# One step of attention and channel mixing, its instructions put in another order on every engine

## The chip, the cores and the metric

The kernel runs on one core of a Trainium2 chip. A core has a matrix engine (TensorE, PE in the profile), a vector engine (VectorE, DVE), an activation engine (ScalarE, ACT), a general engine (GpSimd, POOL) and SyncE (SP), which here only issues transfers. Each engine takes its own instructions in the order in which the program lists them, and waits at an instruction until the semaphores that it names have reached their values. The metric is the device time of one launch in microseconds, the median of several runs.

## The reference

The input `x` is 4096 tokens of 256 features. One layer of attention (16 query heads in 4 groups, head size 16, each token sees itself and the 127 before it) is followed by a residual sum and a layer norm; then a channel mix, again with residual and layer norm.

```python
q = (x @ Wq + bq);  k = (x @ Wk + bk);  v = (x @ Wv + bv)
scores = einsum(q, k) / sqrt(16)
scores = where((i - 128 >= j) | (i < j), -1e9, scores)
x = layernorm(x + softmax(scores) @ v @ Wo + bo)
x_prev = x shifted by one token
xr = mu_r * x + (1 - mu_r) * x_prev;  xk = mu_k * x + (1 - mu_k) * x_prev
r = sigmoid(xr @ W_r.T);  k_act = square(relu(xk @ W_k.T))
out = layernorm(x + r * (k_act @ W_v.T))
```

## The kernel before, in words

The 4096 tokens are 32 blocks of 128 (index `t`), four blocks to a superblock (index `s`, place `j` from 0 to 3). Queries and keys are split into bf16 parts, written to DRAM (`q_parts`, `k_parts`), and read back stacked in another layout (`qs`, `ks`).

A software pipeline runs over the blocks. In step `t` the engines work on seven blocks at once:

- block `t+2`: its key windows are copied (`window_copy`, four pieces, ScalarE) and its queries are tiled (`tile_q`, VectorE, waits for the stacked `qs`);
- block `t+1`: row maxima of the scores (`max_scores` 0 to 5 on TensorE, `tile_max` 0 to 5 and `turn_max` on VectorE), sent as two rows into `qs` by SyncE (`max_in`);
- block `t`: eight score products (`score` 0 to 7, TensorE, two banks in turn), eight exponentials (`exps`, ScalarE), eight triangular masks (`mask`, GpSimd); `x_plus_bo`;
- block `t-1`: product with the values (`values`, TensorE, needs all eight masks), `att_t_copy`, `turn_back`, `normalise`, `turn_attention`, `att_c_copy`;
- block `t-2`: `output_product`, `first_residual` with its moments, `first_rstd` (GpSimd), `first_norm` (ScalarE), `turn_x2`, `x2_t_copy`;
- block `t-3`: `difference` (GpSimd), `mixed`, `r_product`, `tanh`, `k_product`, `relu`, `square`;
- blocks `t-4` and `t-5`: `second_product`, `gate`, `second_residual`, `second_rstd`, then `second_norm` and `store`.

A projection of a later superblock is spread over the four steps in three pieces, `project_chunk` 0 and 1 at j = 3 and 2 at j = 0, with `v_turn` at j = 1; each piece brings a `high_part` and a `middle_part` on ScalarE, a `rest_part` on VectorE, a `low_part` on GpSimd and spills on SyncE, and after them come the stacks, `stack_k` and `stack_q`.

The order is written out by hand: each engine has a function `step` whose calls are its order in a step, and a function `finish` for what is left after the last step. `run` calls `step` for every block but the last (31, named `LAST`) and then `finish`. Two orders matter in what follows. On ScalarE (lines 829 to 878) the exponentials 0 to 3 stand together, then two window copies, and the output norm `second_norm` stands after the fourth window copy. On TensorE (lines 1455 to 1507) `k_product` comes after `score` 6 and waits for `tanh`; `second_product` comes after `max_scores` 1 and waits for `square`.

## Time and profile before

| quantity | value |
|---|---|
| median of 3 runs | 392.55 us (391.89 to 393.45) |
| the profiled execution | 394.04 us, its span 392.2 us |
| busy share of the span: PE, DVE, ACT, POOL | 93%, 84%, 86%, 74% |
| mean granted TensorE clock | 0.978 of full speed |

The span is the time from the first instruction to the last of this execution. The pipeline fills until about 60 us and drains from about 350 us; between them the same four steps repeat. In that stretch three engines are busy almost without a pause, so a share alone doesn't tell which of them sets the pace: the starts of their instructions must be read one after another, since durations overlap (a matmul's 0.38 us begins 0.22 us after the one before it).

### The profile page before, as it was taken

What the parts mean: (1) busy time and instruction counts of PE and PEld (TensorE: products, weight loads), DVE (VectorE), ACT (ScalarE), POOL (GpSimd) and SP (SyncE); (2) the same over time, 40 slices, a digit from 0 to 9 for tenths busy, and PEclk for the clock granted to TensorE, in tenths of its full rate; (3) what the DMA queues carried; (4) which work ended last, traced back from release to release, by engine and by line L of the source; (5) the groups of instructions that cost most, each with busy time, mean ns of one, the idle gap of its engine ahead of it and who ended that gap; (6) DMA issues with size and microseconds to landing.
All of it is one profiled execution on the core that took longest, in us unless ns stands there. A gap on an engine that the chain in (4) does not pass through costs nothing.

```text
span 392.2 us, 8166 instructions
## 1 busy us (share of the span) xinstructions
PE 365.8 (93%) x2339; PEld 228.1 (58%) x2340; DVE 327.7 (84%) x860; ACT 339.0 (86%) x697; POOL 290.8 (74%) x485
## 2 busy tenths in 40 slices
PE   8855889999999999999999999999999998998974
PEld 5432346666566666666566666666566666665552
DVE  6366767999899989999799989999899988997664
ACT  3346999999999999999999999999999998986753
POOL 3704777787699778987699768887699777788733
PEclk9995799999999999999999999999999999999998
DMA  7846587622965347622954257531764252000001
GB/s 260 172 110 125 111 212 164 116 41 56 166 154 80 80 71 180 119 58 55 182 137 97 64 87 187 99 73 42 131 142 94 55 96 55 16 15 18 27 15 40
DMA packets 51244, 39.24 MB, mean 100 GB/s; under 512 B 33088, under 2 KB 42880, under 8 KB 51072
## 3 DMA queue, kind: packets, MB, share of 16 engines
q1 hardware_dynamic: 50240, 36.91, 44.2%
q10 hardware_dynamic: 960, 1.81, 1.8%
q8 instruction: 19, 0.31, 0.3%
q14 instruction: 25, 0.20, 0.2%
HBM read 26.38 MB, written 12.06 MB: 98 GB/s over the span
## 4 chain that ended last, share of the span: by engine, by line
PE 62%; ACT 20%; DMA 6%; DVE 5%; issue 4%; SPq 2%; POOL 1%; POOLq 0%; DVEq 0%; ACTq 0%
PE av_ps L1332 13%; PE score_ps L1312 10%; PE gen L1351 8%; PE gen L1422 7%; PE proj_ps L1229 6%; ACT probs L696 5%; PE max_ps L1294 5%; DMA qs<-q_parts 3%; PE gen L1409 3%; PE gen L1392 3%; ACT windows L711 2%; ACT x L731 2%; ACT out_t L769 2%; ACT act_k L761 2%; PE av_ps L1367 1%
## 5 line engine op out<-in xcount | busy, mean ns | idle before, releaser
L510 POOL TENSOR_SCALAR_AFFINE_SELECT probs<-probs 128x512 f32<-128x512 f32 x252 | 164.8, 671 | 53.1 <-ACT probs L696 51.8
L696 ACT ACTIVATE probs<-score_ps 128x512 f32<-128x512 f32 x252 | 142.6, 593 | 14.9 <-PE score_ps L1312 14.0
L973 DVE TENSOR_REDUCE neg_max<-max_ps 128x3 f32<-128x480 f32 x146 | 88.6, 631 | 13.0 <-PE max_ps L1294 12.7
L1312 PE MATMUL score_ps<-qs,ks 98*128 98x512 bf16 x252 | 88.2, 390 | 4.8 <-ACT probs L696 2.6
L711 ACT COPY windows<-ks 96x640 bf16<-96x640 bf16 x124 | 86.9, 727 | 0.0
L1332 PE MATMUL av_ps<-probs,vals 128*32 128x512 f32 x488 | 59.9, 606 | 0.0
L1014 DVE SCALAR_TENSOR_TENSOR mix<-diff,first,x_t 128x128 f32<-128x128 f32 x128 | 52.9, 456 | 3.2 <-POOL diff L538 3.2
L1294 PE MATMUL max_ps<-windows,q_tiles 128*128 128x160 bf16 x420 | 50.5, 237 | 3.3 <-DVE q_tiles L965 2.3
L1294 PEld LDWEIGHTS max_ps<-windows,q_tiles 128*128 128x128 bf16 x420 | 36.0, 99 | 23.4 <-issue 4.5
L1312 PEld LDWEIGHTS score_ps<-qs,ks 98*128 98x128 bf16 x252 | 21.3, 98 | 41.7 <-issue 30.4
L517 POOL TENSOR_TENSOR rstd<-var,minus_half 128x1 f32<-128x1 f32 x64 | 35.5, 555 | 9.9 <-DVE var L997 9.7
L1351 PE MATMUL gen<-rest_w,act_k 128*128 128x256 f32 x128 | 35.5, 400 | 2.1 <-ACT act_k L761 1.3
L1422 PE MATMUL gen<-rest_w,att_c 128*128 128x256 f32 x128 | 34.3, 390 | 1.8 <-ACT att_c L721 1.8
L498 POOL TENSOR_TENSOR parts<-rest,parts 128x512 bf16<-128x512 f32 (+1 forms) x24 | 26.6, 1111 | 12.1 <-ACT parts L675 12.0
L1229 PE MATMUL proj_ps<-x_t,first 128*128 128x512 f32 (+1 forms) x76 | 35.1, 584 | 0.0
L1409 PEld LDWEIGHTS gen<-mix,rest_w 128*128 128x128 f32 x224 | 28.1, 191 | 8.9 <-issue 8.2
L1409 PE MATMUL gen<-mix,rest_w 128*128 128x128 f32 x224 | 30.7, 280 | 0.0
L992 DVE BATCH_NORM_STATS2 stats<-y 128x6 f32<-128x256 f32 x64 | 27.4, 428 | 2.2
L1392 PE MATMUL gen<-rest_w,mix 128*128 128x256 f32 x112 | 28.8, 379 | 0.0
L1332 PEld LDWEIGHTS av_ps<-probs,vals 128*32 128x32 f32 x488 | 12.6, 109 | 26.7 <-issue 22.8
L538 POOL TENSOR_TENSOR diff<-x_t 128x256 f32<-128x256 f32 x32 | 19.6, 613 | 11.0 <-DVE x_t L1004 7.7
L1351 PEld LDWEIGHTS gen<-rest_w,act_k 128*128 128x128 f32 x128 | 21.9, 189 | 8.0 <-ACT act_k L761 5.7
(112 smaller groups left out, 612.7 us busy)
## 6 DMA issues: line engine op xcount, KB each, us to landing
q_parts<-parts SPq DMA_DIRECT2D x42, 128.0 KB, 2.2
out<-out_t SPq DMA_DIRECT2D x32, 128.0 KB, 2.3
qs<-q_parts SPq DMA_DIRECT2D x7, 576.0 KB, 7.1
x_t<-x_feat SPq DMA_DIRECT2D x7, 512.0 KB, 9.3
x_in<-x_nat SPq DMA_DIRECT2D x7, 512.0 KB, 3.7
ks<-k_parts SPq DMA_DIRECT2D x42, 80.0 KB, 3.3
qs<-q_parts SPq DMA_DIRECT2D x8, 384.0 KB, 8.4
qs<-q_parts SPq DMA_DIRECT2D x14, 192.0 KB, 6.1
```

What stands on the lines that cost most here:

```text
L510: nc.gpsimd.affine_select(out=v, in_=v, compare_op=ALU.is_ge if i % 2 else ALU.is_gt, fill=0.0, base=0, pattern=[[0, HPG], [sign, BLK]], c ...
L696: nc.scalar.activation(probs[:, buf, i], score_ps[i % 2][:, :], ACT.Exp, scale=SCALE).then_inc(s_exp, 1)
L711: nc.scalar.copy(windows[0:ROWS, j % 2, g:g + n], sliding(par, j, g, n)).then_inc(s_window, 1)
L973: nc.vector.tensor_reduce(neg_max[:, TPB * i:TPB * i + n], max_bank(t, j, i)[:, 0:n * TILE_KEYS].rearrange("p (n k) -> p n k", k=TILE_KEYS ...
L1014: nc.vector.scalar_tensor_tensor(out=mix[:, w, c], in0=diff[:, c], scalar=small_cols[:, MU_COL + w * DC + c:MU_COL + w * DC + c + 1], in1= ...
L1229: ins = nc.tensor.matmul((ps or proj_ps)[:, q], wqkv[:, c, m * P:(m + 1) * P], x_t[:, par, c, q], start=(c == 0), stop=(c == DC - 1))
L1294: ins = nc.tensor.matmul(dst, q_tiles[:, j % 2, tile], windows[:, j % 2, g, n], start=(k == 0 and later(t, 1)), stop=(k == len(tiles) - 1) ...
L1312: nc.tensor.matmul(score_ps[i % 2][:, :].rearrange("p (h q) -> p h q", q=BLK), ks[0:ROWS + MPARTS, par, g, k0:k0 + BLK], qs[0:ROWS + MPART ...
L1332: ins = nc.tensor.matmul(value_bank(t)[g * VCOL:(g + 1) * VCOL, :], vals[:, pk, jk, g, :], probs[:, j % 2, 2 * g + half], start=(half == 0 ...
L1351: ins = nc.tensor.matmul(gen0[:, 0:D], act_k[:, c], w_t[:, 2, c], start=(c == 0), stop=(c == DC - 1))
L1409: ins = nc.tensor.matmul(k_bank(u)[:, o * BLK:(o + 1) * BLK], w_t[:, 1, c, o * P:(o + 1) * P], mix[:, 1, c], start=(c == 0), stop=(c == DC ...
L1422: ins = nc.tensor.matmul(gen1[:, 0:D], att_c[:, c], wo[:, c], start=(c == 0), stop=(c == DC - 1))
```

## The change

The calls in every engine's `step` are put in another order; nothing is computed differently. The activations `x2` get five buffers where there were three, and `tanh_r` two where there was one. The loop now covers the blocks up to 29, and blocks 30 and 31 are written out in `finish`, each engine with its own order. The diff shows what changes in the steps; the new `finish` functions are lists of calls of the same kind, and of those only the order around the places that matter is told: TensorE there issues score 0 and 1 of block 31 before the output product of block 29, and after the values product of block 31 it issues `r_product(29)` (before: `k_product(29)`), `turn_back(31)`, `turn_x2(30)`, `second_product(29)`, `turn_attention(31)`, `output_product(31)`.

```diff
--- before.py
+++ after.py
...
 X_BO = 3
+X_ROWS = 5
...
-        x2 = sb("x2", [P, 3, D])
+        x2 = sb("x2", [P, X_ROWS, D])
...
-        tanh_r = sb("tanh_r", [P, D])
+        tanh_r = [sb(f"tanh_r_{i}", [P, D]) for i in range(2)]
...
-                for j in range(SB_BLKS if left else SB_BLKS - 1):
+                for j in range(SB_BLKS if left else SB_BLKS - 2):
...
             def step(s, j, par, project, coming, maxima, scores):
                 t = s * SB_BLKS + j
+                ahead = project and later(s, 1)
 
                 if j == 3 and s + 3 < NSB:
                     load_x(s + 3, 1 - par)
-                ahead = project and later(s, 1)
                 if ahead and j == 0:
                     spill_k(s + 1)
-                    spill_q(s + 1, 1 - par, 0)
-                    stack_k(s + 1, 1 - par)
                 if maxima:
                     max_in(t + 1, *at(j, par, 1))
                 if ahead and j == 0:
+                    spill_q(s + 1, 1 - par, 0)
+                    stack_k(s + 1, 1 - par)
+                if s == 0 and j == 1:
+                    spill_q(1, 1, 1)
+                if ahead and j == 0:
                     spill_q(s + 1, 1 - par, 1)
+                if project and j == 2:
+                    stack_q(s + 1, 1 - par, slice(1, SB_BLKS), s_stack)
+                if behind(t, j, scores, 5):
+                    store(t - 5, (j - 5) % 2)
                 if s == 0 and j == 0:
                     stack_k(1, 1)
-                    spill_q(1, 1, 0)
-                if s == 0 and j == 1:
-                    spill_q(1, 1, 1)
-                if project and j == 2:
-                    stack_q(s + 1, 1 - par, slice(1, SB_BLKS), s_stack)
                 if project and j == 1:
-                    stack_q(s + 1, 1 - par, slice(0, 1), s_stack0)
+                    if s == 0:
+                        load_x(2, 0)
                 if coming and j == 3:
                     load_rows(s + 2, par)
                 if project and j == 1:
+                    stack_q(s + 1, 1 - par, slice(0, 1), s_stack0)
+                if project and j == 1:
                     if s == 0:
-                        load_x(2, 0)
                         load_rows(1, 1)
-                if behind(t, j, scores, 5):
-                    store(t - 5, (j - 5) % 2)
+                if s == 0 and j == 0:
+                    spill_q(1, 1, 0)
 
...
                 f2, f3, f4 = (behind(t, j, scores, n) for n in (2, 3, 4))
 
+                if f3:
+                    difference(t - 3)
+                if f2 and t < NBLK:
+                    x_plus_bo(t)
+                if scores and t:
+                    mask(t, 2, j % 2)
                 if ahead and j == 0:
                     low_part(s + 1, 1)
-                if f3:
-                    difference(t - 3)
-                if scores:
-                    mask(t, 1, j % 2)
-                if scores and t:
-                    mask(t, 2, j % 2)
                 if f2:
                     first_rstd(t - 2)
                 if scores and t:
                     mask(t, 0, j % 2)
-                if f2 and t < NBLK:
-                    x_plus_bo(t)
+                if s == 0 and j == 0:
+                    x_plus_bo(0)
                 if scores:
+                    mask(t, 3, j % 2)
                     mask(t, 5, j % 2)
                 if scores and t:
                     mask(t, 4, j % 2)
+                    mask(t, 6, j % 2)
                 if scores:
-                    mask(t, 3, j % 2)
+                    mask(t, 1, j % 2)
                 if coming and j == 3:
                     low_part(s + 2, 0)
-                if scores and t:
-                    mask(t, 6, j % 2)
+                if ahead and j == 0:
+                    low_part(s + 1, 2)
+                if scores:
+                    mask(t, 7, j % 2)
+                if s == 0 and j == 0:
+                    low_part(1, 1)
+                    x_plus_bo(1)
                 if f4:
                     second_rstd(t - 4)
-                if scores:
-                    mask(t, 7, j % 2)
-                if ahead and j == 0:
-                    low_part(s + 1, 2)
                 if s == 0 and j == 0:
-                    x_plus_bo(0)
-                    x_plus_bo(1)
-                    low_part(1, 1)
                     low_part(1, 2)
...
-                if u >= 3:
-
-                    act.wait_ge(s_x2tr, u - 2)
-                    act.wait_ge(s_y2, u - 2)
-                nc.scalar.activation(x2[:, u % 3], y1[:, :], ACT.Identity, bias=shift1[:, 0:1],
+                if u >= X_ROWS:
+
+                    act.wait_ge(s_x2tr, u - X_ROWS + 1)
+                    act.wait_ge(s_y2, u - X_ROWS + 1)
+                nc.scalar.activation(x2[:, u % X_ROWS], y1[:, :], ACT.Identity, bias=shift1[:, 0:1],
...
-                    act.wait_ge(s_gated, u)
-                nc.scalar.activation(tanh_r[:, :], r_bank(u)[:, 0:D], ACT.Tanh, scale=0.5).then_inc(s_tanh, 1)
+                    act.wait_ge(s_gated, u - 1)
+                nc.scalar.activation(tanh_r[u % 2][:, :], r_bank(u)[:, 0:D], ACT.Tanh, scale=0.5).then_inc(s_tanh, 1)
...
+                if u > LAST - 5:
+                    act.wait_ge(s_act_k, u)
...
+                if u > LAST - 5:
+                    act.wait_ge(s_v, u)
...
-                if ahead and j == 0:
-                    middle_part(s + 1, 1)
                 if more:
                     window_copy(t + 2, s2, j2, p2, 0)
                 if coming and j == 3:
@@ -836,29 +861,32 @@
                     exps(t, 0, j % 2)
                 if scores:
                     exps(t, 1, j % 2)
+                if ahead and j == 0:
+                    middle_part(s + 1, 1)
+                if more:
+                    window_copy(t + 2, s2, j2, p2, 1)
                 if scores and t:
                     exps(t, 2, j % 2)
                 if scores:
                     exps(t, 3, j % 2)
                 if more:
-                    window_copy(t + 2, s2, j2, p2, 1)
                     window_copy(t + 2, s2, j2, p2, 2)
+                if f5:
+                    second_norm(t - 5)
                 if f1:
                     att_t_copy(t - 1)
+                if scores and t:
+                    exps(t, 4, j % 2)
                 if f2:
                     first_norm(t - 2)
-                if scores and t:
-                    exps(t, 4, j % 2)
                 if f3:
                     tanh(t - 3)
                 if scores:
                     exps(t, 5, j % 2)
+                if more:
+                    window_copy(t + 2, s2, j2, p2, 3)
                 if coming and j == 3:
                     middle_part(s + 2, 0)
-                if more:
-                    window_copy(t + 2, s2, j2, p2, 3)
-                if f5:
-                    second_norm(t - 5)
                 if ahead and j == 0:
                     high_part(s + 1, 2)
                 if scores and t:
@@ -868,54 +896,72 @@
                 if f3:
                     relu(t - 3)
                     square(t - 3)
+                if s == 0 and j == 0:
+                    high_part(1, 2, av_ps)
+                if f1:
+                    att_c_copy(t - 1)
+                if ahead and j == 0:
+                    middle_part(s + 1, 2)
                 if scores:
                     exps(t, 7, j % 2)
+                if s == 0 and j == 0:
+                    middle_part(1, 1)
                 if f2:
                     x2_t_copy(t - 2)
-                if ahead and j == 0:
-                    middle_part(s + 1, 2)
-                if f1:
-                    att_c_copy(t - 1)
                 if s == 0 and j == 0:
-                    high_part(1, 2, av_ps)
-                    middle_part(1, 1)
                     middle_part(1, 2)
 
...
                 if maxima:
                     tile_max(t + 1, jn, 0)
                     tile_max(t + 1, jn, 1)
-                    tile_max(t + 1, jn, 2)
                 if f3:
                     token_before(t - 3)
                 if maxima:
+                    tile_max(t + 1, jn, 2)
                     tile_max(t + 1, jn, 3)
                 if f2:
                     first_residual(t - 2)
@@ -1138,54 +1184,69 @@
                     gate(t - 4)
                 if f3:
                     mixed(t - 3, 0)
+                if maxima:
+                    tile_max(t + 1, jn, 4)
                 if coming and j == 3:
                     rest_part(s + 2, 0)
                 if maxima:
-                    tile_max(t + 1, jn, 4)
                     tile_max(t + 1, jn, 5)
                 if f3:
                     mixed(t - 3, 1)
                 if maxima:
                     turn_max(t + 1, j + 1)
+                if f1:
+                    normalise(t - 1)
                 if maxima and (project or j < SB_BLKS - 2):
                     tile_q(t + 2, s if j < SB_BLKS - 2 else s + 1, *at(j, par, 2))
-                if f1:
-                    normalise(t - 1)
                 if f4:
                     second_residual(t - 4)
+                if ahead and j == 1:
+                    val_copy(s + 1, 1 - par)
                 if ahead and j == 0:
                     rest_part(s + 1, 2)
                 if coming and j == 3:
                     rest_part(s + 2, 1)
-                if ahead and j == 1:
-                    val_copy(s + 1, 1 - par)
                 if s == 0 and j == 0:
-                    val_copy(1, 1)
                     rest_part(1, 1, gen1)
                     rest_part(1, 2, av_ps)
+                    val_copy(1, 1)
...
-                if maxima:
-                    max_scores(t + 1, jn, pn, 0, s, project)
                 if coming and j == 3:
                     project_chunk(s + 2, 0, par)
                 if maxima:
+                    max_scores(t + 1, jn, pn, 0, s, project)
                     max_scores(t + 1, jn, pn, 1, s, project)
...
@@ -1474,21 +1534,22 @@
                     score(t, j, par, 2)
                 if maxima:
                     max_scores(t + 1, jn, pn, 4, s, project)
+                    max_scores(t + 1, jn, pn, 5, s, project)
                 if scores:
                     score(t, j, par, 3)
-                if maxima:
-                    max_scores(t + 1, jn, pn, 5, s, project)
                 if f1:
                     values(t - 1, jv, pv, 0)
                     values(t - 1, jv, pv, 1)
                 if scores and t:
                     score(t, j, par, 4)
+                if f3:
+                    r_product(t - 3)
                 if scores:
                     score(t, j, par, 5)
-                if f3:
-                    r_product(t - 3)
                 if f1:
                     turn_back(t - 1)
+                if ahead and j == 1:
+                    v_turn(s + 1)
                 if ahead and j == 0:
                     project_chunk(s + 1, 2, 1 - par)
                 if scores and t:
@@ -1497,48 +1558,69 @@
                     project_chunk(s + 2, 1, par)
                 if f3:
                     k_product(t - 3)
-                if ahead and j == 1:
-                    v_turn(s + 1)
-                if scores:
-                    score(t, j, par, 7)
                 if f2:
                     turn_x2(t - 2)
                 if f1:
                     turn_attention(t - 1)
+                if scores:
+                    score(t, j, par, 7)
```

Three places show what the new order is on an engine. The first is ScalarE (ACT) in the step j = 2 of a middle superblock, from the first exponential on. `probs` is an exponential, `windows` a window copy, `out_t` the output norm, `x` the first norm, `x_t` its transposed copy. Before:

```order
L696 ACTIVATE probs<-score_ps 128x512 x4
L711 COPY windows<-ks 96x640 x2
L716 COPY att_t<-av_ps 128x512
L731 ACTIVATE x<-y,shift,rstd 128x256
L696 ACTIVATE probs<-score_ps 128x512
L750 ACTIVATE tanh_r<-gen 128x256
L696 ACTIVATE probs<-score_ps 128x512
L711 COPY windows<-ks 96x640
L769 ACTIVATE out_t<-y_1,shift_1,rstd_1 128x256
L696 ACTIVATE probs<-score_ps 128x512
L755 ACTIVATE relu_k<-gen 128x256
```

Now:

```order
L719 ACTIVATE probs<-score_ps 128x512 x2
L734 COPY windows<-ks 96x640
L719 ACTIVATE probs<-score_ps 128x512 x2
L734 COPY windows<-ks 96x640
L796 ACTIVATE out_t<-y_1,shift_1,rstd_1 128x256
L739 COPY att_t<-av_ps 128x512
L719 ACTIVATE probs<-score_ps 128x512
L754 ACTIVATE x<-y,shift,rstd 128x256
L773 ACTIVATE tanh_r<-gen 128x256
L719 ACTIVATE probs<-score_ps 128x512
L734 COPY windows<-ks 96x640
L719 ACTIVATE probs<-score_ps 128x512
```

One window copy now stands between the exponentials 1 and 2, and the output norm comes before `att_t` and no longer before exponential 6.

The second is TensorE (PE) in the step j = 1, from the values product on; `gen<-rest_w,mix` is `r_product`, `gen<-mix,rest_w` is `k_product`, `proj_ps<-ident,kv_proj` is `v_turn`, `gen<-ident,x` and `av_ps<-ident,att` are `turn_x2` and `turn_attention`, `gen<-rest_w,act_k` is `second_product`. Before:

```order
L1332 MATMUL av_ps<-probs,vals 32x512 x8
L1312 MATMUL score_ps<-qs,ks 128x512 x2
L1392 MATMUL gen<-rest_w,mix 128x256 x2
L1367 MATMUL av_ps<-ident,att_t 128x128 x4
L1312 MATMUL score_ps<-qs,ks 128x512
L1409 MATMUL gen<-mix,rest_w 128x128 x4
L1247 MATMUL proj_ps<-ident,kv_proj 128x128 x4
L1312 MATMUL score_ps<-qs,ks 128x512
L1359 MATMUL gen<-ident,x 128x128 x2
L1375 MATMUL av_ps<-ident,att 128x128 x2
L1294 MATMUL max_ps<-windows,q_tiles 128x160 x6
L1351 MATMUL gen<-rest_w,act_k 128x256 x2
```

Now:

```order
L1393 MATMUL av_ps<-probs,vals 32x512 x8
L1373 MATMUL score_ps<-qs,ks 128x512
L1453 MATMUL gen<-rest_w,mix 128x256 x2
L1373 MATMUL score_ps<-qs,ks 128x512
L1428 MATMUL av_ps<-ident,att_t 128x128 x4
L1308 MATMUL proj_ps<-ident,kv_proj 128x128 x4
L1373 MATMUL score_ps<-qs,ks 128x512
L1470 MATMUL gen<-mix,rest_w 128x128 x4
L1420 MATMUL gen<-ident,x 128x128 x2
L1436 MATMUL av_ps<-ident,att 128x128 x2
L1373 MATMUL score_ps<-qs,ks 128x512
L1355 MATMUL max_ps<-windows,q_tiles 128x160 x6
```

`v_turn` moved ahead of score 6 and `k_product`, and score 7 behind the two transposes.

The third is GpSimd (POOL) in a step without a `low_part`; `diff` is `difference`, `rstd` with `shift` is the first norm's scale and shift, `rstd_0` with `shift_0` the second norm's. Before:

```order
L538 TENSOR_TENSOR diff<-x_t 128x256
L510 AFFINE_SELECT probs<-probs 128x512 x2
L517 TENSOR_TENSOR rstd<-var,minus_half 128x1
L519 TENSOR_SCALAR shift<-mv,rstd 128x1
L510 AFFINE_SELECT probs<-probs 128x512
L492 TENSOR_TENSOR x_bo<-x_in,rest_w 128x256
L510 AFFINE_SELECT probs<-probs 128x512 x4
L517 TENSOR_TENSOR rstd_0<-var_0,minus_half 128x1
L519 TENSOR_SCALAR shift_0<-mv_0,rstd_0 128x1
L510 AFFINE_SELECT probs<-probs 128x512
```

Now:

```order
L549 TENSOR_TENSOR diff<-x_t 128x256
L503 TENSOR_TENSOR x_bo<-x_in,rest_w 128x256
L521 AFFINE_SELECT probs<-probs 128x512
L528 TENSOR_TENSOR rstd<-var,minus_half 128x1
L530 TENSOR_SCALAR shift<-mv,rstd 128x1
L521 AFFINE_SELECT probs<-probs 128x512 x7
L528 TENSOR_TENSOR rstd_1<-var_1,minus_half 128x1
L530 TENSOR_SCALAR shift_1<-mv_1,rstd_1 128x1
```

`x_bo` now stands ahead of every mask of the step, seven masks stand in one run behind the first norm's scale and shift, and the second norm's comes last.

## Rows read from the trace of the kernel before

**Rows 1.** Busy time by engine in one stretch: us, then PE, PEld, DVE, ACT, POOL, clock, DMA share, GB/s.

```profile
209.00:251.00 42.00, 41.86 (x280) 26.55 (x280) 38.13 (x103) 40.55 (x85) 34.00 (x58) 1.00 0.52 110
```

**Rows 2.** Timeline of PE, one superblock: start us, duration us, instruction.

```profile
209.71 0.58 PE L1294 MATMUL max_ps<-windows,q_tiles 128*128 128x160 bf16 x6
210.14 1.13 PE L1351 MATMUL gen<-rest_w,act_k 128*128 128x256 f32 x4
...
211.96 1.07 PE L1422 MATMUL gen<-rest_w,att_c 128*128 128x256 f32 x4
...
218.65 0.60 PE L1247 MATMUL proj_ps<-ident,kv_proj 128*128 128x128 f32 x4
...
227.52 0.39 PE L1312 MATMUL score_ps<-qs,ks 98*128 98x512 bf16 x1
227.88 1.13 PE L1409 MATMUL gen<-mix,rest_w 128*128 128x128 f32 x8
228.85 0.38 PE L1312 MATMUL score_ps<-qs,ks 98*128 98x512 bf16 x1
229.07 0.38 PE L1359 MATMUL gen<-ident,x 128*128 128x128 f32 x2
...
242.26 0.58 PE L1294 MATMUL max_ps<-windows,q_tiles 128*128 128x160 bf16 x6
242.92 1.13 PE L1351 MATMUL gen<-rest_w,act_k 128*128 128x256 f32 x4
...
255.79 1.07 PE L1422 MATMUL gen<-rest_w,att_c 128*128 128x256 f32 x4
```

**Rows 3.** Timeline of ACT in the step at j = 2, idle time in brackets.

```profile
223.51 1.09 ACT L696 ACTIVATE probs<-score_ps 128x512 f32<-128x512 f32 x2 [0.46 <-PE score_ps L1312]
224.49 1.34 ACT L711 COPY windows<-ks 96x640 bf16<-96x640 bf16 x2
...
227.36 0.38 ACT L750 ACTIVATE tanh_r<-gen 128x256 f32<-128x256 f32 x1
...
230.11 0.42 ACT L761 ACTIVATE act_k<-relu_k 128x256 f32<-128x256 f32 x1
```

**Rows 4.** Timeline of DVE, the second pair of mixes in two steps.

```profile
226.25 1.08 DVE L1014 SCALAR_TENSOR_TENSOR mix<-diff,first,x_t 128x128 f32<-128x128 f32 x2
...
238.16 0.61 DVE L1014 SCALAR_TENSOR_TENSOR mix<-diff,first,x_t 128x128 f32<-128x128 f32 x2
```

**Rows 5.** Timeline of DVE in the step at j = 2, the first residual.

```profile
223.30 0.42 DVE L1059 TENSOR_TENSOR y<-gen,x_bo 128x256 f32<-128x256 f32 x1
```

**Rows 6.** Timeline of POOL in that step, and one low part after it.

```profile
225.49 0.26 POOL L519 TENSOR_SCALAR shift<-mv,rstd 128x1 f32<-128x1 f32 x1
...
226.31 0.88 POOL L492 TENSOR_TENSOR x_bo<-x_in,rest_w 128x256 f32<-128x256 f32 x1
228.66 2.58 POOL L510 TENSOR_SCALAR_AFFINE_SELECT probs<-probs 128x512 f32<-128x512 f32 x4 [1.48 <-ACT probs L696]
...
241.84 1.16 POOL L498 TENSOR_TENSOR parts<-rest,parts 128x512 bf16<-128x512 f32 x1
```

**Rows 7.** Timeline of DVE near 327 us.

```profile
326.90 1.05 DVE L965 COPY q_tiles<-qs 96x2048 bf16<-96x2048 bf16 x1 [0.82 <-DMA qs<-q_parts]
```

**Rows 8.** Timeline of PE there and in the last steps.

```profile
328.63 0.44 PE L1375 MATMUL av_ps<-ident,att 128*128 128x128 f32 x2 [1.36 <-DVE att L1048]
...
339.48 1.13 PE L1351 MATMUL gen<-rest_w,act_k 128*128 128x256 f32 x4 [0.35 <-ACT act_k L761]
...
349.68 1.13 PE L1351 MATMUL gen<-rest_w,act_k 128*128 128x256 f32 x4 [0.49 <-ACT act_k L761]
...
360.31 1.13 PE L1422 MATMUL gen<-rest_w,att_c 128*128 128x256 f32 x4 [1.32 <-ACT att_c L721]
...
375.80 0.44 PE L1359 MATMUL gen<-ident,x 128*128 128x128 f32 x2 [1.36 <-ACT x L731]
```

**Rows 9.** Timeline of ACT while the pipeline fills.

```profile
39.00 0.62 ACT L675 CAST parts<-rest 128x512 bf16<-128x512 f32 x1 [0.31 <-DVE rest L936]
```

173 lines of the change are left out of this document (122 added, 51 removed).

## The prediction

> **What bounds the kernel now.** I first read the busy time of each engine in a stretch where all steps are alike [rows 1]. PE is busy for 41.86 of 42 us, ACT for 40.55, DVE for 38.13, POOL for 34.00. That ranks them but doesn't say how much PE could give back, since its durations overlap. So next comes PE's timeline, by the starts alone [rows 2]. From one output product (line 1422, step j = 1) to the same one a superblock later it is 255.79 - 211.96 = 43.83 us, or 10.96 per step. Inside it the reader is to look for starts that lie further apart than they need.
>
> Six maxima products take 210.14 - 209.71 = 0.43 us up to the second product behind them where nothing waits, but 242.92 - 242.26 = 0.66 where it waits for `square`: 0.23 lost, and one such wait of nearly the same size comes before step j = 2, so 0.44 in two. A lone score product takes 0.22 up to the next start (228.85 to 229.07), but score 6 takes 0.36 (227.52 to 227.88), because `k_product` behind it waits for `tanh`: 0.14, in the two steps of four that have no projection piece between them (j = 1 and 2), so 0.28. Visible waits are 0.72 us per superblock. The other 43.1 are PE issuing without a pause. PE sets the pace, and what it still loses it loses to ACT.
>
> The timeline of ACT shows where that comes from [rows 3]. ACT stands idle for 0.46 us until score 2, since PE issues the whole output product ahead of score 2. From there it works without a pause through `tanh` (227.36, done 227.74, just before `k_product` at 227.88) to `square` (230.11, done 230.53). So 0.46 us of idle time early in the step is handed on to PE as two smaller waits later in it.
>
> **The change part by part.** All of it is summed against the profiled execution, 394.04 us.
>
> *Middle steps, ACT and PE.* A window copy of 0.67 us (two take 1.34 [rows 3]) now stands in the gap of 0.46 before exponential 2, so ACT no longer idles there and `square` comes up to 0.46 earlier. The output norm moved up within the same stretch, so as many operations stand ahead of `tanh` but one: between the values product and `tanh` there are `att_t`, an exponential and the first norm, as before, and `tanh` stays where it was relative to the values product. The 0.14 of j = 2 therefore stays. In j = 1 `v_turn` (at most 0.60 [rows 2]) now stands ahead of `k_product` and covers it: 0.14 won. But behind `k_product` it used to cover `relu` and `square`; I take the wait there as 0.14 instead of 0.21, 0.07 won. The 0.23 at j = 3 goes, since `square` there is early by more. Sum 0.44 per superblock; what is late next is PE's own issue. Ends: 0.72 (every visible wait) and 0. The steps from block 3 to block 28 are 25, or 6.25 superblocks: **2.8 us**, ends 0 and 4.5.
>
> *The steps without a projection* lose 0.35 and 0.49 us before the second product [rows 8]. The same window copy wins most: **0.6**, ends 0 and 0.84.
>
> *The late tiles at 327 us.* VectorE waited 0.82 us for the stacked queries [rows 7], with `normalise` queued behind the waiting copy, so PE waited 1.36 us for `att` [rows 8]. Now `normalise` comes first. PE's next need is the tiles themselves: they were done at 326.90 + 1.05 = 327.95, and PE went on at 328.63 + 0.27 with the maxima. **0.9**, ends 0 (a transfer that lands later) and 1.36.
>
> *Block 31.* PE waited 1.32 us for `att_c` with nothing else to issue [rows 8]. Score 0 and 1 of block 31 now stand ahead of it. They are 0.44 of work (two of 0.22), and they start ACT's last run of exponentials earlier. Their row maxima must have come by then; in `finish` `turn_max(31)` stands ahead of `first_residual(28)`, so they are sent earlier. **0.9**, ends 0.44 and 1.32.
>
> *The drain.* `turn_x2(30)` waited 1.36 us for the first norm of block 30 with `turn_attention(31)` behind it [rows 8]. Between the values product of block 31 and `turn_back(31)` there is still one product, `r_product` for `k_product`, and `second_product(29)` lies between `turn_x2(30)` and `turn_attention(31)`, while the first norm is being awaited less. **0.5**, ends -0.5 (`first_residual(31)` now stands behind `gate(29)`) and 1.36.
>
> *The fill.* `high_part(1, 2)` now comes before exponential 7 of block 0. The cast at 39.00 waited 0.31 for what follows from it [rows 9]; it comes earlier by that and by one exponential, 0.5 (half of 1.09 [rows 3]): **0.8**, ends 0 and 1.1. Against it SyncE issues `load_x(2)` ahead of the first stacks of superblock 1; what hides their delay is `project_chunk` 0, which now stands ahead of `max_scores` 0, the first user of those tiles.
>
> *At nothing.* SyncE sends `max_in` first and the stacks of keys later: the windows that read them are copied two steps, some 22 us, later. Its `store` ahead of the stacks waits for an output norm that now comes earlier. On GpSimd all eight masks are still done a step ahead of the values product: eight of 0.65 (four take 2.58) are 5.2 us in a step of 10.96, and GpSimd had 1.48 idle in one place [rows 6]. If this cover went, the values product, in the middle of PE's queue, would stop everything. More buffers for `x2` and `tanh_r` only remove waits.
>
> *The wait that the change adds* is on GpSimd. `x_plus_bo(t)` needs `first_residual(t-2)` of the same step and stands ahead of all masks and of the first norm's scale and shift. In the step of j = 2 the residual was done at 223.30 + 0.42 = 223.72 [rows 5]. Then follow `x_bo` 0.88, one mask 0.65, and scale and shift: 0.65 to the start of the shift, by a mask's length as the nearest row, and 0.26 [rows 6]. That gives 226.16. ACT wants the first norm one slot of 0.5 ahead of `tanh`, 226.86 [rows 3]. So 0.7 us to spare. In step j = 0 a low part of 1.16 [rows 6] stands in between, and on ACT a cast and a copy that put the first norm off about as much as is missing. I take 0.
>
> *VectorE.* The second pair of mixes took 1.08 us beside `x_bo` and 0.61 elsewhere [rows 4]. `x_bo` is gone from there, but now a run of seven masks begins there. From the rows the pair costs between 0.61 and 1.08; I take 1.08 as before and count nothing. The Trainium skill (SBUF — State Buffer, "Who interferes with whom") says that a VectorE instruction with two SBUF inputs and a GpSimd instruction that reads SBUF take turns on one port pair for a whole instruction. By that rule the 1.08 stays and the first pair can become as slow: 0.47 more in every step, 1.9 per superblock, for which VectorE has room, 3.87 of 42 us [rows 1], if it falls in the right places.
>
> Sum: 2.8 + 0.6 + 0.9 + 0.9 + 0.5 + 0.8 = 6.5, so 394.04 becomes 387.5. This execution was 1.49 us above the median of the runs, 392.55, so the forecast for a median is **386.0**. The ends sum to 0 and 10.5: 392.6 and 382.1.
>
> **The rivals.**
>
> A. *VectorE takes over in the middle.* If both pairs of mixes and the second residual run beside masks, `mixed`, `normalise` or the maxima come late by what ACT won, and the period stays at 43.83. For it: 38.13 of 42 is already much, and seven masks in a run meet the later half of VectorE's step. Against: 3.87 of 42 idle, and `x_bo` no longer in the way. Then only 0.9 + 0.9 + 0.5 + 0.8 = 3.1 are won: 389.4.
>
> B. *Slower: the first norm waits.* If first residual, `x_bo`, mask, scale and shift end more than 0.7 us later than above, ACT, whose queue carries `tanh` and `square` behind the first norm, stops, and PE with it. Each 0.1 beyond costs 28 steps x 0.1 = 2.8 us; 0.4 beyond gives 11.2 - 6.5 = 4.7 us more than before, 397.3. For it: in j = 0 nothing is to spare. Against: 0.7 in the other three steps.
>
> C. *All visible waits go*, the upper ends: 382.1. For it: ACT has 1.45 of 42 us idle, more than PE loses. Against: PE and ACT wait for each other in turn, and orders that end all of these waits at once are rare.
>
> D. *Nothing moves that waits*: the reordered parts lie under work anyway, and a new wait in the drain eats the fill's gain: 392, no change.
>
> **How the numbers follow.** Forecast 0.48, own range 382.5 to 389.2; A 0.22; B 0.09; C 0.15; D 0.06. The range for 8 in 10 goes from 382.0, taking most of C, to 391.0, taking A and half of D's neighbourhood. About 0.5%, 2 us, is what a measurement here can tell from no change. Faster by more: 0.48 + 0.15 + 0.17 of A = 0.80. Within: 0.05 of A and 0.05 of D = 0.10. Slower: B and the rest, 0.10.
>
> **What would show it.** In the middle: no idle time of ACT before exponential 2; `k_product` directly behind score 6 in j = 1 but still 0.14 late in j = 2; a superblock of 43.4. At about 320 us: `turn_attention` with no wait for `att`. The output product of block 29 behind two scores with under 0.5 of wait. Wrong if a superblock takes 43.8 or more, if ACT's first norm shows a wait for the shift in the middle, if POOL idles before `x_bo` by over 1 us and PE waits for masks, or if PE waits anew in the last 30 us.

## The result and the profile after

The change made the kernel slower: 399.86 us (median of 4 runs, 398.23 to 401.65) against 393.00 (4 runs of before beside them), a ratio of 1.017, with a 95% interval of 1.0095 to 1.024. The forecast was 386.0 and its range ended at 391.0.

The profiled executions have spans of 399.4 and 392.2 us. I cut both at the same three events, the output products (line 1483 in the kernel after) of blocks 0, 24 and 31:

| stretch | before | after | change | forecast |
|---|---|---|---|---|
| start to output product 0 | 48.02 | 48.15 | +0.13 | -0.8 |
| 0 to 24, the steady steps | 261.79 | 270.26 | +8.47 | -2.8 |
| 24 to 31, the late steps | 67.16 | 64.51 | -2.65 | -2.4 |
| 31 to the end | 15.23 | 16.48 | +1.25 | -0.5 |

From output product 28 on the late steps can only be compared as a whole: the new end issues that product two calls later in TensorE's queue, so a cut there isn't at the same work.

So the loss is the steady stretch. Its steps, each named by the step in which the first of two output products stands, took 10.21, 11.25, 11.30 and 11.05 us before (j = 1, 2, 3, 0; means of four superblocks) and 10.86, 11.21, 11.05 and 12.21 after: j = 3 gained 0.25, j = 0 lost 1.16 and j = 1 lost 0.65. The six steps j = 1 of the stretch are not all alike after the change: four take 10.62 us, two 11.02 and 11.19.

The busy times of one superblock, cut at those events, are the view to start with. Columns: stretch, us, then PE, PEld, DVE, ACT, POOL, clock, DMA share, GB/s. Before:

```profile
211.96:222.19 10.23, 10.17 (x75) 6.66 (x73) 9.71 (x27) 10.06 (x22) 8.79 (x16) 1.00 0.41 97
222.19:233.44 11.25, 11.25 (x75) 7.01 (x73) 9.44 (x26) 10.69 (x23) 8.02 (x15) 1.00 0.29 56
233.44:244.74 11.30, 11.22 (x75) 7.10 (x73) 10.42 (x29) 10.74 (x23) 8.94 (x15) 1.00 0.80 181
244.74:255.79 11.05, 11.05 (x76) 7.02 (x73) 10.35 (x27) 10.78 (x23) 10.06 (x17) 1.00 0.56 94
```

After, j = 0 first, and last the stretch of [rows 1]:

```profile
204.85:217.06 12.21, 11.50 (x76) 6.98 (x73) 11.58 (x27) 10.78 (x23) 9.10 (x15) 1.00 0.28 58
217.06:227.67 10.61, 10.14 (x75) 6.49 (x73) 9.77 (x26) 9.92 (x22) 9.75 (x17) 1.00 0.59 130
227.67:238.88 11.21, 11.21 (x76) 7.00 (x73) 9.96 (x28) 10.69 (x23) 8.65 (x16) 1.00 0.32 59
238.88:249.93 11.05, 11.05 (x75) 7.09 (x73) 10.36 (x28) 10.73 (x23) 8.52 (x14) 1.00 0.71 155
...
209.00:251.00 42.00, 41.01 (x266) 26.74 (x267) 38.79 (x99) 39.04 (x82) 33.56 (x57) 1.00 0.50 108
```

At j = 0 VectorE is busy for 11.58 us where it was 10.35, and TensorE, never idle there before, now is. VectorE's idle time before the change was 0.52, 1.81, 0.88 and 0.70 us in the four steps (j = 1, 2, 3, 0): the 3.87 of [rows 1] is no one reserve, and j = 1 and j = 0 have the least.

The timelines of DVE, POOL, PE and ACT in step j = 0 of the kernel after show what became longer:

```profile
207.59 1.81 DVE L1060 SCALAR_TENSOR_TENSOR mix<-diff,first,x_t 128x128 f32<-128x128 f32 x2
210.12 1.42 DVE L1060 SCALAR_TENSOR_TENSOR mix<-diff,first,x_t 128x128 f32<-128x128 f32 x2
212.60 0.87 DVE L1011 COPY q_tiles<-qs 96x2048 bf16<-96x2048 bf16 x1
```
```profile
208.06 1.19 POOL L509 TENSOR_TENSOR parts<-rest,parts 128x512 bf16<-128x512 f32 x1
209.91 0.26 POOL L530 TENSOR_SCALAR shift<-mv,rstd 128x1 f32<-128x1 f32 x1
210.12 1.28 POOL L521 TENSOR_SCALAR_AFFINE_SELECT probs<-probs 128x512 f32<-128x512 f32 x2
```
```profile
209.45 1.13 PE L1453 MATMUL gen<-rest_w,mix 128*128 128x256 f32 x4 [0.64 <-DVE mix L1060]
...
210.64 0.60 PE L1428 MATMUL av_ps<-ident,att_t 128*128 128x128 f32 x4
...
216.17 0.84 PE L1373 MATMUL score_ps<-qs,ks 98*128 98x512 bf16 x2
217.06 1.07 PE L1483 MATMUL gen<-rest_w,att_c 128*128 128x256 f32 x4
```
```profile
210.21 0.60 ACT L754 ACTIVATE x<-y,shift,rstd 128x256 f32<-128x256 f32 x1 [0.32 <-POOL shift L530]
213.00 0.69 ACT L686 ACTIVATE parts<-proj_ps,first 128x512 bf16<-128x512 f32 x1 [0.83 <-PE proj_ps L1290]
215.45 0.62 ACT L698 CAST parts<-rest 128x512 bf16<-128x512 f32 x1 [0.25 <-DVE rest L982]
```

And the same pairs of mixes of the kernel before, in its step j = 0 (output products at 244.74 and 255.79), and then PE's same two places:

```profile
247.48 0.84 DVE L1014 SCALAR_TENSOR_TENSOR mix<-diff,first,x_t 128x128 f32<-128x128 f32 x2
249.03 1.25 DVE L1014 SCALAR_TENSOR_TENSOR mix<-diff,first,x_t 128x128 f32<-128x128 f32 x2
```
```profile
249.62 0.60 PE L1367 MATMUL av_ps<-ident,att_t 128*128 128x128 f32 x4
...
255.15 0.60 PE L1312 MATMUL score_ps<-qs,ks 98*128 98x512 bf16 x2
```

Two pairs of mixes took 2.09 us here and take 3.23. (In the four steps j = 0 of the stretch the two pairs took 2.09 to 2.24 us before, 3.23 or 3.24 after.) The first pair lies beside the end of mask 2 and GpSimd's low part of chunk 1, the second beside masks 0 and 3. The added time of the mixes and that of the step, 1.14 and 1.16, are nearly equal, but not because one is handed on whole to the other. TensorE's starts give two pieces. `turn_back` (`av_ps<-ident,att_t`) begins 4.88 us behind the output product before (249.62 - 244.74) and 5.79 after (210.64 - 204.85): 0.91, all of it behind the first pair alone, for which `r_product`, now moved ahead of score 5, waits 0.64. The other 0.25 comes at the end of the step: the last two scores take 0.84 us instead of 0.60. The second of them waits for exponential 7, which in ScalarE's queue now stands behind the cast of chunk 2, and that cast waits 0.25 us for VectorE's `rest`. ACT's wait of 0.83 for the projection is in part that for the late `r_product` (e8 below, where this is on time, keeps 0.35 of it); its 0.32 for the shift comes from the low part, which now stands ahead of the first norm's scale and shift on GpSimd.

At j = 1 the pairs take 1.03 and 1.42 us (0.61 and 1.09 before), 0.75 more, and VectorE's copy of the values ends 9.70 us behind the output product instead of 8.95. The maxima behind it on TensorE wait:

```profile
226.81 0.38 PE L1355 MATMUL proj_ps<-windows,q_tiles 128*128 128x160 bf16 x3 [0.47 <-DVE vals L999]
...
272.68 0.60 PE L1373 MATMUL score_ps<-qs,ks 98*128 98x512 bf16 x2 [0.40 <-DMA qs<-max_rows]
```

Before, these maxima began 9.36 us behind the output product, 0.41 behind the end of the copy; now they begin 0.06 behind it, at 9.76. So 0.35 of the 0.75 was room, and 0.40 is what an ordinary step j = 1 is longer by (10.62 against 10.21). The second row is from one of the two long ones: there the scores also wait for the row of maxima that SyncE sends, which adds 0.57 us to this step and 0.40 to the other, 1.0 of the 8.5 in all.

Over this superblock (pairs of j = 1, 2, 3, 0) the mixes take 2.45 + 1.60 + 1.21 + 3.24 = 8.50 us instead of 1.68 + 1.69 + 1.22 + 2.09 = 6.68; as means of four superblocks it is 8.49 instead of 6.83.

### The profile page after: what moved, and what is told of

The parts are those of the page before. It is cut to its first block, busy times and chain, and to the rows that moved or that the text cites. A ratio compares the mean times of both kernels' runs of the same rounds, so it can differ in the third digit from the quotient of the medians.

```text
span 399.4 us, 8174 instructions
## 1 busy us (share of the span) xinstructions
PE 369.1 (92%) x2339; PEld 227.3 (57%) x2340; DVE 338.9 (85%) x860; ACT 337.4 (84%) x697; POOL 294.8 (74%) x485
## 3 DMA queue, kind: packets, MB, share of 16 engines
q10 hardware_dynamic: 960, 1.81, 1.7%
## 4 chain that ended last, share of the span: by engine, by line
PE 49%; DVE 33%; issue 6%; DMA 6%; ACT 3%; SPq 1%; POOL 1%; ACTq 0%; DVEq 0%; POOLq 0%
DVE mix L1060 10%; PE score_ps L1373 9%; PE av_ps L1393 7%; PE gen L1483 7%; DVE neg_max L1019 6%; PE proj_ps L1290 5%; PE max_ps L1355 4%; PE gen L1412 3%; DMA qs<-max_rows 3%; DVE stats L1038 3%; PE gen L1470 3%; DVE q_tiles L1011 3%; PE gen L1453 3%; DVE y L1079 2%; DVE y L1105 2%
## 5 line engine op out<-in xcount | busy, mean ns | idle before, releaser
L521 POOL TENSOR_SCALAR_AFFINE_SELECT probs<-probs 128x512 f32<-128x512 f32 x252 | 169.3, 696 | 58.5 <-ACT probs L719 58.4
L719 ACT ACTIVATE probs<-score_ps 128x512 f32<-128x512 f32 x252 | 144.6, 601 | 13.6 <-PE score_ps L1373 13.0
L1373 PE MATMUL score_ps<-qs,ks 98*128 98x512 bf16 x252 | 93.6, 391 | 4.0 <-DMA qs<-max_rows 2.2
L734 ACT COPY windows<-ks 96x640 bf16<-96x640 bf16 x124 | 90.1, 728 | 0.0
L1060 DVE SCALAR_TENSOR_TENSOR mix<-diff,first,x_t 128x128 f32<-128x128 f32 x128 | 63.2, 534 | 2.7 <-POOL diff L549 2.7
L1355 PE MATMUL max_ps<-windows,q_tiles 128*128 128x160 bf16 x420 | 48.9, 237 | 4.9 <-DVE q_tiles L1011 2.5
L1355 PEld LDWEIGHTS max_ps<-windows,q_tiles 128*128 128x128 bf16 x420 | 34.5, 99 | 30.3 <-DVE neg_max L1019 6.8
L1373 PEld LDWEIGHTS score_ps<-qs,ks 98*128 98x128 bf16 x252 | 23.8, 98 | 40.2 <-issue 19.1
L1011 DVE COPY q_tiles<-qs 96x2048 bf16<-96x2048 bf16 x32 | 26.7, 833 | 4.2 <-DMA qs<-q_parts 4.2
L1453 PEld LDWEIGHTS gen<-rest_w,mix 128*128 128x128 f32 x112 | 20.3, 190 | 8.2 <-DVE mix L1060 5.6
```

Of the source, the lines that this page charges most:

```text
L521: nc.gpsimd.affine_select(out=v, in_=v, compare_op=ALU.is_ge if i % 2 else ALU.is_gt, fill=0.0, base=0, pattern=[[0, HPG], [sign, BLK]], c ...
L719: nc.scalar.activation(probs[:, buf, i], score_ps[i % 2][:, :], ACT.Exp, scale=SCALE).then_inc(s_exp, 1)
L734: nc.scalar.copy(windows[0:ROWS, j % 2, g:g + n], sliding(par, j, g, n)).then_inc(s_window, 1)
L1060: nc.vector.scalar_tensor_tensor(out=mix[:, w, c], in0=diff[:, c], scalar=small_cols[:, MU_COL + w * DC + c:MU_COL + w * DC + c + 1], in1= ...
L1355: ins = nc.tensor.matmul(dst, q_tiles[:, j % 2, tile], windows[:, j % 2, g, n], start=(k == 0 and later(t, 1)), stop=(k == len(tiles) - 1) ...
L1373: nc.tensor.matmul(score_ps[i % 2][:, :].rearrange("p (h q) -> p h q", q=BLK), ks[0:ROWS + MPARTS, par, g, k0:k0 + BLK], qs[0:ROWS + MPART ...
```

## The experiments

The kernel before, run beside each group, took 393.43, 393.81 and 393.41 us. Ratios are to it, with a 95% interval; "steps" are the means for j = 1, 2, 3, 0 and "steady" is the second row of the table above (261.79 before, 270.26 after). Each of these splits is of the one execution that was profiled.

**One engine's order.** Three kernels with the new step of one engine taken out or put in (e1, e2, e4), and one with a single call moved (e3).

e1: the kernel after, GpSimd's steady step as before.

```diff
-    difference; x_plus_bo; mask 2; low_part(s + 1, 1); first_rstd; mask 0; 3, 5, 4, 6, 1; low_part(s + 1, 2); 7; second_rstd
+    low_part(s + 1, 1); difference; mask 1, 2; first_rstd; mask 0; x_plus_bo; 5, 4, 3, 6; second_rstd; 7; low_part(s + 1, 2)
```

> The changed kernel with GpSimd's step put back in its old order; all else as changed. P (GpSimd's operations now lie beside VectorE's mixes and stretch them; a step at j = 0 has 3.24 us of mixes where it had 2.09): the mixes of j = 0 fall back to 2.1 us, r_product waits for them no longer, the step from j = 0 to j = 1 falls from 12.2 to about 11.1 us, and the time to 388 to 394. Q (the loss comes from the new order on TensorE and VectorE themselves: r_product ahead of score 5, v_turn and the copy of the values, the tiles behind normalise): the step at j = 0 stays near 12 and the time at 397 or more.

Measured: 404.9 us, 1.029 (1.0227 to 1.0352), steps 10.76, 11.20, 11.05, 12.80. Worse, not better, and no test of the mixes: the low part now stands first in GpSimd's queue and waits 0.68 us for ScalarE's cast, which the change had put behind exponential 1; the difference and both pairs of mixes (1.34 and 1.51 us) come behind it.

e2: the kernel before with GpSimd's new step (the same diff the other way).

> The kernel before with GpSimd's step in the new order and nothing else. P: the mixes get longer here too, above all at j = 0, and the time rises by 1 to 6 us over before (394 to 399), less than in the changed kernel, since r_product stands one score later in this order. Q: within 1 us of before, 392 to 394.

Measured: 405.72 us, 1.0313 (1.0275 to 1.035), steps 10.22, 11.25, 11.31, 12.73. This doesn't test the mixes. TensorE's waits between 83 and 335 us (total, times, longest) and SyncE's queue show another cause, the rows of maxima that arrive late:

```profile
PE score_ps L1312 <- DMA qs<-max_rows: 5.7, 5, 1.7
```
```profile
209.60 1.51 SPq L346 DMA_DIRECT2D q_parts<-parts  x3
211.22 4.50 SPq L368 DMA_DIRECT2D ks<-k_parts  x6
215.81 1.13 SPq L410 DMA_DIRECT2D qs<-max_rows  x2
```

The maxima's rows leave SyncE behind the stacks of keys, which wait for the low part that GpSimd now makes later. In the changed kernel SyncE sends them first. So GpSimd's order needs SyncE's new order with it, as the change has them; that the two alone would do was not run.

e3: the kernel after, only the low part of chunk 1 back at the head of GpSimd's step.

```diff
+    low_part(s + 1, 1)          # j = 0
     difference; x_plus_bo; mask 2
-    low_part(s + 1, 1)
```

> The changed kernel with one call moved: low_part(s + 1, 1), a two-input operation of 1.15 us, back to the head of GpSimd's step at j = 0, so that it no longer starts in the middle of the first pair of mixes (1.81 us). P: that pair falls to 0.6 to 1.1 us, r_product's wait of 0.65 us goes, j = 0 wins 0.6 to 0.9 us six times, and the time is 394 to 396. Q: unchanged within 1 us.

Measured: 401.24 us, 1.0199 (1.0167 to 1.0232), j = 0 12.31. No cure: the low part waits 0.71 us for the cast and ends at 207.82, so VectorE waits 0.39 us for the difference and the first mixes start 3.21 us behind the output product instead of 2.74. They then take 1.43 us instead of 1.81, and end 0.09 us later than in the kernel after.

e4: the kernel before with ScalarE's new step alone.

```diff
-    middle_part(s + 1, 1); window_copy 0; exps 0, 1, 2, 3; window_copy 1, 2; ...; exps 7; x2_t_copy; middle_part(s + 1, 2)
+    window_copy 0; exps 0, 1; middle_part(s + 1, 1); window_copy 1; exps 2, 3; window_copy 2; second_norm; ...; middle_part(s + 1, 2); exps 7; x2_t_copy
```

> The kernel before with ScalarE's step in the new order and nothing else: what my forecast counted for the middle (a window copy in the gap before exponential 2). If that step of the prediction holds by itself: the gap of 0.46 us is gone, the superblock falls from 43.83 to 43.2 to 43.5, and the time is 388.5 to 391.5. If TensorE and ScalarE only wait for each other elsewhere: 392 to 394. If the later first norm costs: over 394.

Measured: 401.55 us, 1.0198 (1.0178 to 1.0218), steps 10.29, 11.31, 11.04, 12.82, and two steps without a projection of 9.72 us against 10.20. The window copy does at least what was forecast where there is no projection; at j = 0 ScalarE's order by itself costs 1.77 us. The timelines of POOL and ACT in that step:

```profile
206.53 1.17 POOL L498 TENSOR_TENSOR parts<-rest,parts 128x512 bf16<-128x512 f32 x1 [0.76 <-ACT parts L675]
207.66 0.62 POOL L538 TENSOR_TENSOR diff<-x_t 128x256 f32<-128x256 f32 x1
```
```profile
216.30 0.62 ACT L675 CAST parts<-rest 128x512 bf16<-128x512 f32 x1 [1.08 <-DVE rest L939]
```

Two casts are left as suspects: chunk 1's, behind exponential 1, and chunk 2's, ahead of exponential 7.

**The two casts.** e5: the kernel after, chunk 2's cast and low part back in their old places (behind exponential 7, behind mask 7).

```diff
-    middle_part(s + 1, 2); exps 7; x2_t_copy         # ScalarE
+    exps 7; x2_t_copy; middle_part(s + 1, 2)
-    low_part(s + 1, 2); mask 7                       # GpSimd
+    mask 7; low_part(s + 1, 2)
```

> The changed kernel, with one thing of step j = 0 put back: ScalarE's middle part of chunk 2 behind exponential 7 and the x2 turned copy (as before the change), and GpSimd's low part of chunk 2 behind mask 7. Theory R (ScalarE's cast of chunk 2 waits for VectorE's rest and holds back exponential 7, for which the next step's scores wait): the step j = 0 to 1 falls from 12.2 us by the part of it that lies in that wait, 0.3 to 0.8 us, six times: 395 to 398 us against the changed kernel's 399.9. Theory P (the mixes are stretched beside GpSimd's low part and the lateness starts there): at most 0.2 us a step, 399 to 400 us.

Measured: 402.07 us, 1.0203 (1.0154 to 1.0252). Step j = 0 falls to 11.97 and j = 1 rises to 11.04; the steady stretch is 270.33. Nothing won.

e6: the kernel after, chunk 1's cast and low part back at the heads of their steps (GpSimd's as in e3), chunk 2's as changed.

```diff
+    middle_part(s + 1, 1)                            # ScalarE
     window_copy 0; exps 0, 1
-    middle_part(s + 1, 1)
```

> The changed kernel with chunk 1's two parts of step j = 0 back at the heads of their steps (ScalarE's cast and GpSimd's low part) and chunk 2's left as changed. e5 put only chunk 2's back and gained nothing; e7 put both back and gained 3 us. Theory R1 (chunk 1's cast behind exponential 1 puts GpSimd's low part beside VectorE's first mixes and the shift late): most of e7's gain is here, the step j = 0 to 1 11.3 to 11.6 us against 12.2, the kernel 395 to 397 us. Theory R2 (only both together help, since exponential 7 waits for chunk 2's cast): 12.0 us or more and 399 us.

Measured: 396.58 us, 1.0068 (1.0044 to 1.0093), j = 0 11.67, j = 1 10.64, steady 265.89: 4.4 us won by this pair of moves, where the low part alone (e3) won nothing.

e7: both pairs back (e5 and e6 together).

> The kernel of e5, and ScalarE's middle part of chunk 1 back at the head of step j = 0, with GpSimd's low part of chunk 1 back at its head too. Theory R: both casts now lie where they were before the change, so the step j = 0 to 1 goes back to 11.0 to 11.3 us and the kernel to 392 to 394 us. Theory P as far as the low part lies beside other work of VectorE: the first pair of mixes falls from 1.8 us to 1.1 at j = 0, and the same 392 to 394 us; e3, which moved GpSimd's low part alone, has not shown it, so under P alone e7 stays at 398 us or more.

Measured: 396.66 us, 1.0073 (1.0039 to 1.0107), steps 11.03, 11.21, 11.05, 11.33, steady 266.33. Chunk 2's cast wins 0.34 us at j = 0, so in e6 it holds back exponential 7 there, and 0.39 is lost at j = 1. That 0.39 isn't the cast itself: `q_tiles`, VectorE's copy of the queries, takes 1.03 us in e5 and e7 where it took 0.68 in the kernel after and in e6, and the values are late by that. My expectation of 392 to 394 missed what is left.

e9: e4 with both casts in their old places.

> The kernel before with ScalarE's new steady step as in e4, but with both middle parts of step j = 0 in their old places (head of the step; behind the x2 turned copy). Theory R: e4's 12.82 us for the step j = 0 to 1 falls to 11.0 to 11.3, and since e4's steps without a projection took 9.72 instead of 10.20 us, the kernel comes to 391 to 394 us. Rival (another move of ScalarE's costs the step: high part of chunk 2 ahead of exponential 6, the first norm behind exponential 4): the step stays over 12.0 us and the kernel over 397 us.

Measured: 392.72 us, 0.9963 (0.9929 to 0.9997), steps 10.23, 11.31, 11.10, 11.16, late steps 66.28 instead of 67.16. ScalarE's other moves cost nothing in sum (j = 3 gains 0.20, j = 2 and j = 0 give it back) and gain only in the late steps.

**The low part beside the mixes.** e8: the kernel after; from superblock 2 on the low part of chunk 1 is a fill of the same tile, so the low part of k is left out.

```diff
-    tensor_tensor(parts[low], rest, parts[middle], subtract)
+    memset(parts[low], 0.0)
```

> The changed kernel with the low part of chunk 1 from superblock 2 on replaced by a fill of the same tile (leaves the low part of k out: its subtraction of two operands is not made). Theory P: the first pair of mixes at j = 0, 1.81 us beside the subtraction, falls to 0.9 to 1.2 us, the first norm's wait for shift 0.32 goes, and the step j = 0 to 1 falls by 0.5 to 0.8 us (396 to 397 us). Theory R: the mixes may get shorter, but exponential 7 still waits for the cast of chunk 2, and the step falls by under 0.3 us (398.5 to 400 us).

Measured: 396.15 us, 1.0063 (1.0034 to 1.0092), j = 0 11.60 and steady 266.33. DVE's mixes in that step:

```profile
204.78 0.91 DVE L1063 SCALAR_TENSOR_TENSOR mix<-diff,first,x_t 128x128 f32<-128x128 f32 x2
206.41 0.60 DVE L1063 SCALAR_TENSOR_TENSOR mix<-diff,first,x_t 128x128 f32<-128x128 f32 x2
```

Chunk 1's cast stays where the change put it, and the steady stretch is shorter by nearly as much as in e6 (3.9 against 4.4 us). The first pair begins 2.74 us behind the output product as before, and takes 0.91 us instead of 1.81, so what lengthens it is the subtraction beside it and not a late start; `r_product` no longer waits. (The fill is also shorter, 0.52 us for 1.19, so the masks behind it move too.) But this wins only 0.61 of the 1.16 us at j = 0, though the mixes, 1.51 us instead of 3.23, are now shorter than before the change. ACT and then PE at the end of such a step show what the other 0.55 is:

```profile
212.04 0.62 ACT L701 CAST parts<-rest 128x512 bf16<-128x512 f32 x1 [0.55 <-DVE rest L985]
212.56 0.59 ACT L722 ACTIVATE probs<-score_ps 128x512 f32<-128x512 f32 x1
```
```profile
213.21 0.39 PE L1376 MATMUL score_ps<-qs,ks 98*128 98x512 bf16 x1 [0.37 <-ACT probs L722]
```

The cast of chunk 2, which the change put ahead of exponential 7, waits for `rest`, and TensorE for the exponential. So two placements cost at j = 0: the subtraction beside the first mixes, and this cast. In the kernel after, where TensorE is late already, the second adds 0.25 us.

**What is left at j = 1.** e11: e7, and VectorE copies the values ahead of the second residual.

```diff
-    second_residual(t - 4); val_copy(s + 1)
+    val_copy(s + 1); second_residual(t - 4)
```

> e7 with VectorE's copy of the values ahead of the second residual at j = 1 (it was behind it, before the change too). The TensorE wait for vals at j = 1, 3.4 us over 6 superblocks in e7, goes: by that alone the step j = 1 to 2 falls from 11.04 to 10.4 to 10.5 us, and the kernel from 396.7 to 393 to 394 us. If the wait isn't on the path (something behind it is as late): no change from e7.

Measured: 393.82 us, 0.9999 (0.9968 to 1.003), j = 1 10.62, steady 264.23: the wait for the values was on the path, and VectorE was late for it.

e10: e7, with TensorE's and VectorE's steady steps as before the change. e12: e10, with GpSimd's too.

```diff
# e12 against e10, GpSimd's step
-    difference; x_plus_bo; mask 2; first_rstd; mask 0, 3, 5, 4, 6, 1, 7; second_rstd
+    difference; mask 1, 2; first_rstd; mask 0; x_plus_bo; mask 5, 4, 3, 6; second_rstd; mask 7
```

> e7 (both casts and low parts back) with the steady steps of TensorE and VectorE as before the change; ScalarE's, GpSimd's and SyncE's steps and all ends as changed. Theory P (GpSimd's new order lays masks beside VectorE's mixes, which makes them 1.4 us where x_bo makes them 1.1, so VectorE's tail, the copy of the values at j = 1 among it, is late): TensorE's wait for the values stays, the step j = 1 to 2 10.6 to 11.0 us, superblock 44.3 to 44.7, kernel 395 to 397 us. Theory Q (TensorE's or VectorE's own new order makes the wait): the step j = 1 to 2 goes to 10.2 to 10.3, kernel 391 to 393 us.

> e10 with GpSimd's steady step as before the change too: what is left of the change is ScalarE's steady step (with both casts of j = 0 in their old places), SyncE's step, and the ends of all engines. Theory P: the mixes go back to about 1.7 us a step (0.8 to 0.6 and 1.1), the step j = 1 to 2 is 10.2 us, a superblock 43.7 us, the chunkless steps 9.7 to 9.9 and the end 1 to 2 us shorter: 389 to 391.5 us, below the kernel before (393.8). Theory Q: the same as e10 within 0.3%.

Measured: e10 395.78 us, 1.0053 (1.0012 to 1.0095), steps 11.05, 11.25, 11.05, 11.09, steady 265.34; e12 391.81 us, 0.995 (0.9923 to 0.9977), just above the 389 to 391.5 expected, steps 10.24, 11.31, 11.10, 11.23, steady 262.11. The queue of VectorE is the same in both, and so is TensorE's; only GpSimd's differs. DVE at j = 1 in e10, then in e12:

```profile
216.47 1.09 DVE L1060 SCALAR_TENSOR_TENSOR mix<-diff,first,x_t 128x128 f32<-128x128 f32 x2
218.29 1.43 DVE L1060 SCALAR_TENSOR_TENSOR mix<-diff,first,x_t 128x128 f32<-128x128 f32 x2
220.19 1.03 DVE L1011 COPY q_tiles<-qs 96x2048 bf16<-96x2048 bf16 x1
```
```profile
214.75 0.80 DVE L1060 SCALAR_TENSOR_TENSOR mix<-diff,first,x_t 128x128 f32<-128x128 f32 x2
216.28 1.25 DVE L1060 SCALAR_TENSOR_TENSOR mix<-diff,first,x_t 128x128 f32<-128x128 f32 x2
218.00 0.65 DVE L1011 COPY q_tiles<-qs 96x2048 bf16<-96x2048 bf16 x1
```

3.55 against 2.70 us: 0.85 more, 0.47 of it the mixes and 0.38 the copy `q_tiles`, and the step is 0.81 longer (11.05 against 10.24). VectorE has no wait between those rows. This is the cleanest pair of the study, and e12, which keeps ScalarE's window copies, SyncE's step and the written-out end, is a little faster than the kernel before.

## Why the prediction was wrong

**The step that failed is "VectorE".** It let the second pair of mixes cost "between 0.61 and 1.08", took 1.08 and counted nothing, and let the first pair stay as it was. "0.61 elsewhere" was already wrong for the kernel before, whose second pair took 1.25 us at j = 0; [rows 4] show only j = 2 and j = 3. After the change the second pair took 1.42 at j = 1 and j = 0 (0.98 and 0.60 at j = 2 and 3), the first 1.03 and 1.81. The sentence beside it, on the Trainium skill (SBUF — State Buffer, "Who interferes with whom"), gave 0.47 more in every step, 1.9 per superblock. The trace bears out that mixes get longer beside GpSimd; that the sum agrees, 8.50 - 6.68 = 1.82, is luck, since it is 0.77 and 1.15 in two steps and nothing in the other two.

I then let it vanish in VectorE's 3.87 of 42 us, with the proviso "if it falls in the right places". It did not. Even the idle time of the same step is no measure of the room: at j = 1 that was 0.52 us, but 0.25 of it stood ahead of the mixes, and the room between the copy of the values and its first user was 0.35; 0.75 more of mixes cost 0.40. At j = 0 `r_product` had lost the cover of score 5, and 0.91 of the first pair's growth came through. e8 shows the longer mixes as the cause at j = 0, e10 against e12 at j = 1. Rival A had the mechanism, but ended at "the period stays at 43.83": it had no loss in it. The loss that I did price, B, hung on the shift, which made the first norm wait 0.32 us at j = 0 only.

**"In step j = 0 ... I take 0"** failed with it. The change's two placements there, ScalarE's cast behind exponential 1 and the low part behind mask 2, put the subtraction beside the mixes: 4.4 us of the 8.5 (e6). From there chunk 2's old place loses 0.4 (e6 to e7), the old orders of TensorE and VectorE win 1.0 (e7 to e10), GpSimd's in all steps 3.2 (e10 to e12), and 0.3 remains to before. This is one path of several, of single profiled executions, and it is not what each part costs in the kernel after: `q_tiles` takes 1.03 us in e7 and e10 and 0.68 in the kernel after, so nearly half of GpSimd's 3.2 and the lost 0.4 are that copy.

**"At nothing", SyncE.** The forecast let `max_in` first in SyncE's queue cost nothing. In two of six steps j = 1 the rows it sends came late, 1.0 us in all. VectorE turns these maxima (`max_rows`) 0.76 us later than before, behind the longer mixes, but it does so in all six steps; why two are late and the others not stays open.

**"Middle steps", 2.8 us.** ACT no longer idles before score 2 [rows 3]; at j = 2 it now waits 0.66 us for score 0 instead. Step j = 3 gained 0.25 where 0.23 was said, and `k_product` stands directly behind score 6 at j = 1 and late at j = 2, as said. What that would win at j = 1 can't be told behind the late copy of the values. e12, in which the mixes of a superblock take 7.3 us (6.8 before, 8.5 after), is not below before in the steady stretch (262.11 and 261.79): what ScalarE's order gains at j = 3 it gives back at j = 0 and 2. But e12 has TensorE's old order, so it doesn't test the 0.21 us that `v_turn` was to win. At j = 1 little more could have been won: the copy of the values left 0.35 us of room before the change.

**"Steps without a projection", "late tiles", "block 31".** 2.4 forecast, 2.65 measured. The step from output product 26 fell from 10.21 to 9.88 (0.33 of the 0.6 forecast for two); the second one holds the moved output product and can't be read alone, but `second_product` comes 0.49 us earlier there too. e4 shows that ScalarE's order does it, and a little more with the old orders of the others (9.72). The tiles, for [rows 7, 8]: `turn_attention` no longer waits 1.36 us for `att`, and that step fell from 11.07 to 9.88, but the step ahead of it, in which TensorE now waits 0.63 us for a row maximum, rose from 10.21 to 10.76: 0.64 for both, where 0.9 was forecast. TensorE's wait of 1.32 for `att_c` at block 31 is gone.

**"The fill".** The wait of the cast [rows 9] is gone, but the first output product came at 48.15 instead of 48.02, and between 47.6 and 48.6 in e5 to e8, e10 and e11, whose fill is nearly that of the changed kernel. The 0.8 can't be told from that.

**"The drain".** Forecast 0.5 won with a lower end of 0.5 lost, measured 1.25 lost in that execution. The wait of 1.36 us for the first norm of block 30 is gone, but TensorE now waits 1.49 us for that of block 31 (0.52 before), and 0.81 for its mixes. PE and its granted clock at the end of the kernel after, then PE in e7, which has the same order there:

```profile
387.29 0.44 PE L1420 MATMUL gen<-ident,x 128*128 128x128 f32 x2 [1.49 <-ACT x L754]
387.60 1.13 PE L1412 MATMUL gen<-rest_w,act_k 128*128 128x256 f32 x4
389.54 2.08 PE L1470 MATMUL max_ps<-mix,rest_w 128*128 128x128 f32 x8 [0.81 <-DVE mix L1060]
391.41 1.60 PE L1453 MATMUL max_ps<-rest_w,mix 128*128 128x256 f32 x4
```
```profile
385.11 1.16 PE L1470 MATMUL max_ps<-mix,rest_w 128*128 128x128 f32 x8 [0.81 <-DVE mix L1060]
386.10 1.03 PE L1453 MATMUL max_ps<-rest_w,mix 128*128 128x256 f32 x4
```

Their windows, columns as above, the clock in the third place from the end, after and then e7:

```profile
390.00:392.00 2.00, 2.00 (x10) 1.91 (x10) 1.44 (x6) 0.29 (x1) 0.31 (x1) 0.50 0.00 0
```
```profile
385.00:387.00 2.00, 1.89 (x12) 1.57 (x12) 1.86 (x7) 0.54 (x2) 0.00 (x0) 1.00 0.19 66
```

In the kernel after, TensorE ran these two products at its lower level (0.50, 1.2 GHz), behind waits of 1.49 and 0.81 us; in e7 it stayed at 2.4 GHz behind the same ones, and 31 to the end took 15.51 us. So the order itself loses 0.2 to 0.3 us, and about 1 us more goes when the clock is low in these products: with the new end that is so in the profiled executions of after, e1, e3, e5, e8 and e12, not in those of e6, e7, e10 and e11; with the old end (before, e2, e4, e9) e2's alone has TensorE's products behind output product 31 partly at the lower level, and takes 16.2 us there instead of 15.2. Whether the new end makes it likelier, so few executions don't settle.

## What to carry to other kernels

Before letting a slower operation hide in an engine's idle time, measure the room where it is needed: from the end of the last operation behind it that another engine uses to the start of that user. VectorE's 3.9 us of 42 were 0.5 in the step, and 0.35 in front of the copy's user. When an order changes, list for each two-operand operation of VectorE what GpSimd runs beside it before and after, in every step of the cycle, and price it by the longest neighbour seen, not by the present one. Shortening one such operation shows the next wait behind it (e8), so read what is left before calling the cause whole. An order of one engine is right only with the others' (e1, e2 and e4 ran 2 to 3% longer than the kernel before), so test such a table in pairs that hand work to each other.

## What was not expected

A pair of mixes took 0.61 us at best [rows 4], 1.08 beside `x_bo`, 1.25 beside a mask and `x_bo`, 1.42 beside two masks and 1.81 beside the end of a mask and the subtraction. A copy with one SBUF input stretched too, but not always: at j = 1 `q_tiles` took 0.65 us when it began before the run of masks (e12), 1.03 when it began 0.14 to 0.73 us into it (e10, e7), and yet 0.68 when it began 0.56 us into it (the kernel after). What decides between these was not tested.
